# Routing of the first seven tiles in one step, their rows moved from there on, and the weights asked for earlier

## The reference

```python
x = x + _L0_gnn_ref(_layernorm(x), edge_index, edge_type_64, ...)
x = x + _L0_ffn_ref(_layernorm(x)[None], Wr, br, ln_g, ln_b, W1, b1, W2, b2)[0]

def _L0_ffn_ref(x, Wr, br, ln_g, ln_b, W1, b1, W2, b2):
    logits = xt @ Wr + br
    top_p, top_idx = jax.lax.top_k(softmax(logits), 2)
    weights = top_p / top_p.sum(-1)
    xn = (xt - mu) * rsqrt(var + eps)
    h = gelu((xn * ln_g[e] + ln_b[e]) @ W1[e] + b1[e])      # 256 -> 1024, expert e
    y = h @ W2[e] + b2[e]                                   # 1024 -> 256
    out = sum of weights * y over the two chosen experts
```

## Time and profile before

| | |
|---|---|
| median of three runs | 3764.64 us (3761.67 to 3767.57) |
| the profiled execution | 3765.22 us |
| its span, first to last instruction | 3763.4 us |
| PE busy | 2924.2 us (78%) |
| DVE busy | 1675.9 us (45%) |
| ACT busy | 1452.9 us (39%) |
| POOL busy | 1904.0 us (51%) |
| mean granted TensorE clock | 0.872 of full speed |
| step 9 to the first work on block 0 | 2784.67 to 2841.51 us of the trace |

### The profile page before, as it was taken

One profiled execution on the slowest core, in us unless ns is written; L12 is line 12 of the kernel. 1 busy time (PEld: TensorE's weight loads), 2 busy tenths in 40 slices (PEclk: granted clock), 3 DMA queues, 4 the chain that ended last, 5 costly groups with the idle time before them and its releaser, 6 DMA issues. The chain is left out here.

```text
span 3763.4 us, 77621 instructions
## 1 busy us (share of the span) xinstructions
PE 2924.2 (78%) x21213; PEld 2095.5 (56%) x21213; DVE 1675.9 (45%) x6070; ACT 1452.9 (39%) x4666; POOL 1904.0 (51%) x2003
## 2 busy tenths in 40 slices
PE   8687777777777777777777777777757999999998
PEld 7454444444444444444444444444446888889898
DVE  7244444444444444444444444444476554563222
ACT  5343333333333333333333333333335655564332
POOL 6355555555555555555555555555434434432322
PEclk9898888888888888888888888888858999999999
DMA  7566666666666666666666666666476666666665
GB/s 230 165 171 191 184 187 184 190 189 187 184 184 188 189 188 184 187 184 191 188 183 187 184 191 189 185 187 184 138 232 191 200 199 195 197 182 184 188 183 133
DMA packets 295467, 701.49 MB, mean 186 GB/s; under 512 B 47432, under 2 KB 143071, under 8 KB 295188
## 3 DMA queue, kind: packets, MB, share of 16 engines
q0 software_dynamic: 151104, 456.15, 43.5%
q1 hardware_dynamic: 144212, 243.57, 21.2%
HBM read 633.18 MB, written 66.36 MB: 186 GB/s over the span
## 5 line engine op out<-in xcount | busy, mean ns | idle before, releaser
L260 POOL DMA_INDIRECT e_kv<-d_kv,idx x1566 | 1486.4, 949 | 1140.2 <-PE psA L544 690.3
L426 DVE TENSOR_REDUCE e_small<-psD 128x1 f32<-128x384 f32 x261 | 145.5, 557 | 1255.8 <-remote 1250.6
L502 PE MATMUL psK<-consts,e_kv 128*128 128x128 f32 x3132 | 604.3, 316 | 90.8 <-issue 84.2
L353 ACT ACTIVATE e_prob<-psD,e_small 128x384 f32<-128x384 f32 x261 | 151.5, 580 | 1321.4 <-DVE e_small L432 1309.8
L544 PE MATMUL psA<-e_kv,e_probT 128*32 128x128 f32 x6264 | 441.2, 290 | 219.8 <-issue 218.6
L502 PEld LDWEIGHTS psK<-consts,e_kv 128*128 128x128 f32 x3132 | 432.2, 162 | 143.0 <-issue 137.9
L578 PE MATMUL psP<-consts,e_prob 128*128 128x128 f32 x783 | 177.2, 346 | 349.5 <-ACT e_prob L353 349.5
L1600 POOL DMA_INDIRECT out<-f_y,f_whose x105 | 165.8, 1579 | 554.1 <-DVE f_y L1978 387.8
L2146 PE MATMUL f_psY<-f_w,f_hT 128*128 x1680 | 395.1, 389 | 40.0 <-ACT f_hT L1668 34.0
L544 PEld LDWEIGHTS psA<-e_kv,e_probT 128*32 128x32 f32 x6264 | 181.3, 110 | 429.1 <-issue 401.6
L2133 PE MATMUL f_psH<-f_xT,f_w 128*128 128x128 f32 x3360 | 404.3, 280 | 0.9 <-DVE f_xT L1966 0.9
(11 more groups left out here) (309 smaller groups left out, 4108.3 us busy)
## 6 DMA issues: line engine op xcount, KB each, us to landing
f_w<-in_W SPq DMA_DIRECT2D x113, 1024.0 KB
e_rows<-d_feat SPq DMA_DIRECT2D x174, 288.0 KB
e_kv<-d_kv,idx POOLq DMA_INDIRECT x1566
d_accs<-e_accs SPq DMA_DIRECT2D x348, 48.8 KB
f_xs<-d_xs SPq DMA_DIRECT2D x105, 132.5 KB
d_kv<-p_kv SPq DMA_DIRECT2D x48, 256.0 KB, 2.1
p_x<-in_x SPq DMA_DIRECT2D x49, 128.0 KB, 2.8
n_v<-d_kv SPq DMA_DIRECT2D x49, 128.0 KB
```

What stands on the lines that cost most here:

```text
L260: pool.indirect_dma_start(out=kv[g.slot][:, t, :], out_offset=None, in_=kv_dram[:, :], in_offset=bass.IndirectOffsetOnAxis(ap=idx[g.slot][ ...
L502: mm = pe.transpose(psK[:, half, t * P:(t + 1) * P], kv[a.slot][:, third * TS + t, half * P:(half + 1) * P], ident)
```

## The change

Six things move, all in `finish`:

- For the first batch R and S are both laid in step 9 (`FIRST`), in one row of operations, and T in step 10. The later batches stay as they were.
- Its rows are moved in steps 9, 10 and 11 in place of 11, 12 and 13. POOL's gathers of steps 10 and 11 are put behind the moves of step 11.
- ACT's work for the batch (the square root for `r2`, the exponential for `odds`) comes at the end of step 9, and PE's count behind the projection and the turns of step 9.
- W2's eight loads are asked for in steps 2, 3 and 5 to 10 (before: 2, 4, 5, 7, 8, 10, 11, 13).
- W1 of blocks 0, 1 and 2 is asked for in steps 11, 12 and 13, one each (before: all three in step 13), and the rows of block 0 in step 13 (before: 14).
- `PLAIN` goes from 15 to 23, so that in eight more steps PE adds the bias and POOL does not.

```diff
+    placed_at = lambda s: 0 if s == FIRST else batch(s, S_AT) or None
+    listed_at = lambda s: 0 if s == FIRST + 1 else batch(s, T_AT) or None
     R_AT, S_AT, T_AT = 3, 4, 5
-    PLAIN = START
-    W2_AT = {2 + (3 * e + 1) // 2: e for e in range(NX)}
+    FIRST = B - 1 + R_AT
+    LATE = (FIRST + 1, FIRST + 2)
+    PLAIN = START + B + 1
+    W2_AT = {s: e for e, s in enumerate((2, 3, 5, 6, 7, 8, 9, 10))}
...
-            moved.setdefault(k * B + B - 1 + T_AT + j // 3, []).append(k * B + j)
+            moved.setdefault((k * B + B - 1 + T_AT if k else FIRST) + j // 3, []).append(k * B + j)
...
-        weighed.setdefault(START - 2 if b < RW else step_of(b) - 1, []).append(b)
+        weighed.setdefault(LATE[-1] + b if b < RW else step_of(b) - 1, []).append(b)
...
-        fetched.setdefault(step_of(b) - 1, []).append(b)
+        fetched.setdefault(step_of(b) - (1 if b else 2), []).append(b)
...
-                if tile(s + 5) is not None:
+                if tile(s + 5) is not None and s not in LATE:
                     gather(s + 5)
...
+                if s == LATE[-1]:
+                    for g in LATE:
+                        gather(g + 5)
...
+                if k is not None and not here:
+                    second_factor()
+                    gate(k)
                 if not here:
                     sent(s)
...
+                if s == FIRST:
+                    first_rows = itertools.chain(routes, picks, puts)
+                    parts = [sums, itertools.chain(first, then), first_rows, first_rows, first_rows]
...
-                    count(s)
                     project(tile(s))
                     turn(s, 1)
+                    count(s)
```

More of the change, by code:

```diff
@@ L1641, in gate @@
             def gate(k):
+                table(ACT.Exp)
                 act.wait_ge(s_b["R"], (k + 1) * BATCH_OPS["R"])
-                table(ACT.Exp)
                 act.activation(odds[:, 0, :], gap[:, :], ACT.Exp).then_inc(s_gate, 1)
@@ L1696, in _ @@
                 here = BLOCKS_OF.get(s, [])
-                k = batch(s, S_AT)
+                k = placed_at(s)
                 t, b, d, n = tile(s), tile(s - 1), tile(s - 2), tile(s + 1)
@@ L1702, in _, with second_factor @@
                     copied(0, 0)
[L1703 to L1707, removed]
+                def second_factor():
                     now = slice(k * B, k * B + B)
@@ L1710, in _ @@
                     act.activation(r2[:, 2, now], r2[:, 1, now], ACT.Sqrt, bias=cst("eps")).then_inc(s_sd[2], 1)
+                if b is not None or k is not None:
+                    table(ACT.Sqrt)
+                if k is not None and here:
+                    second_factor()
                 if b is not None and here:
@@ L1989, in _ @@
                         pass
[L1990 to L1993, removed]
                 here = BLOCKS_OF.get(s, [])
@@ L2001, in _ @@
                     pass
-                kr, ks, kt = batch(s, R_AT), batch(s, S_AT), batch(s, T_AT)
+                kr, ks, kt = batch(s, R_AT), placed_at(s), listed_at(s)
                 picks = iter(()) if kr is None else chain(s_b["R"], kr * BATCH_OPS["R"], BATCH_OPS["R"], chosen(kr))
```

## The result

| | before | after |
|---|---|---|
| median, 12 runs each on one chip | 3765.39 us (3756.42 to 3770.04) | 3756.11 us (3748.96 to 3761.48) |
| the profiled execution | 3765.22 us | 3752.74 us |
| its span | 3763.4 us | 3750.4 us |
| PE busy | 2924.2 us | 2928.6 us |

The ratio is 0.9976, with a 95% interval from 0.9967 to 0.9985: 9.3 us faster. The forecast was 3758.3 us in a range of 3751 to 3767. It was right in the stage and right in the total, but inside the stage two of its terms were off and cancelled each other, and the term for the bias was wrong.

What follows compares the result with a forecast made beforehand. From step 9 to block 0 no engine is full, so the order of work decides. Terms leave 12.1 us; less 7.0 for late signals, plus 1.2, gives 6.3: median 3764.64 to 3758.3 us, range 3751 to 3767.

Steps and rivals of the forecast that it cites:

- Steps 9 to 11: DVE's steps with R and S together, then T: 12.25, 10.4 and 5.1 us, 27.7 against 26.8, 0.9 lost.
- Rival four: S's wait for PE and ACT in step 9 is 4 us longer: 3762.3 us; chance 0.18 together with rival two.
- The table load: ACT in step 9: 1.28 us with no drain after it; the skill's drain would add some 1.4 us.
- POOL: DVE waits for `alone` of tiles 13 and 14, behind the moves, in steps 12 and 13: 0.8 + 0.4 = 1.2 us.
- The fetch of block 0: Ahead of block 0: asked for in step 13, it no longer waits for the moves, and some 5 us go.
- The late signals: PE's signals to ACT, steps 11 to 14: two of three return beside moves and W1 loads, 2 x 3.5 = 7.0 us.
- Rival three: Signals late in every step with moves beside loads, steps 10 to 14: 14.1 us slower, 3778.7 us; chance 0.09.
- Rival two: All three late signals return, perhaps at a place in ACT's program: 3763.0 us; chance 0.18 together with rival four.
- Rival one: Late signals go altogether, as W1 no longer comes in one 3 MB lump: 12.1 us won, 3752.5 us; chance 0.23.
- The bias: Steps 15 to 22: eight matmuls of 0.20 us on PE in place of POOL's additions, 1.6 us lost.
- W2 in consecutive steps: W2's loads on the DMA queues, 1.71 MB a step: taken as 0; 1.6 us if only 320 GB/s went through.

Runs made afterwards that it cites:

- e1_lump: The changed kernel with W1 of blocks 0 to 2 asked for together in step 13, as before, on the fast chip: 3086.86 us, ratio 0.9975.
- e3_routing_only: The kernel before with only the routing and moves as changed; W1, W2, block 0's fetch and `PLAIN` old; fast chip: 3095.03 us, ratio 1.0006.
- the three kernels of the first group: On the fast chip, the changed kernel with W1 together in step 13, W2's old steps, or W1 together in step 14: 3086.86, 3087.86, 3089.26 us.
- e7_apart: The changed kernel with W1 of blocks 0 to 2 in step 14, behind block 0's fetch, on a slower chip: 3798.48 us, ratio 0.9984.
- e5_plain: The changed kernel with POOL adding the bias from step 15 on, as before (`PLAIN = START`): 3801.59 us, ratio 0.9981.
- after_b: The changed kernel, unchanged, run again for a trace on the chip of the second group of runs: 3799.84 us, ratio 0.9977.

## Why the prediction was right, point by point

**Steps 9 to 11: right in kind, 1.9 us too cheap.** Step 9 was put at 12.25 us and took 13.53 (13.37 to 13.56 in the other traces of the changed order); step 10 at 10.4 and took 10.79; step 11 at 5.1 and took 5.26. Of the 1.28 us in step 9 the rows show 0.66: the wait for the count is 1.19 and not 0.8, and `odds`, costed at nothing, holds DVE for 0.27. The rest lies in no single row. Rival four (4 us more) did not come.

**The table load: the row decided rightly.** The load starts 0.01 us behind the end of ACT's operation before it, and the exponential at 2792.27, 0.02 us behind the load's end at 2792.25. A drain of 1.38 us, which the Trainium skill states in "ScalarE: Activation LUTs", section "What ACT_TABLE_LOAD costs", is not to be seen here; by it the wait of 0.27 would have been some 1.6, an estimate.

**POOL: right, and half as dear.** In the changed kernel's trace the slow stretch covers it: the 0.53 us of idle time ahead of DVE's operation behind `alone` of tile 13 end 0.44 us after `alone` has. `e1_lump`, where nothing is late, shows it: DVE waited 0.32 and 0.30 us for the two, and steps 12 and 13 took 5.32 and 5.47 us, 0.6 us over two plain steps, for 1.2 predicted.

**The fetch of block 0: needed, but on a misread row, and for a reason that I had not priced.** I gave it 5 us, what was left of the 15.9 beside the late signals, and explained it by a wait of 7.8 us for the moves. That wait is the second batch's; the first batch's was 2.75 us, and from its start the rows took 7.9 us to land, 4.27 of them in the transfer. SP came to it only at 2833.50. Ahead of it stood its instructions for the three loads of W1, in pieces of 0.70 us; from the first issue to the last they took 8.59 us, against 2.72 in `e3_routing_only` on the fast chip. How much of the 5 us the earlier fetch won on the first chip no run shows. On the fast chip `e3_routing_only` shows that the other edits hang on it: left in step 14, behind W1, it costs 11.7 us in the stage and 8.2 in the median, where the gain is 7.2. I had named the order on SP but did not price a fetch behind W1.

**The late signals: right in kind, too dear, and with the wrong cause; that the total came out is in part luck.** Without late signals the prediction has 2827.8 - 2783.0 = 44.8 us from step 9 to block 0; the three kernels of the first group with the fetch in step 13 took 46.2 to 46.5 (1.9 us more in steps 9 to 11, 0.6 less for POOL). The changed kernel took 50.75, so its late signals cost 4.4 us (4.9 and 5.4 in the two other traces) where I had 7.0 - 1.2 = 5.8. An error of some +1.5 and one of -1.4 cancel: 50.6 us follow from the prediction, 50.75 were measured, and 7.75 us were won for 7.9 predicted. The 4.4 us do not all stand in "remote": 3.52 do, and the rest in gaps of about 1 us on DVE. As cause I took moves beside megabyte loads, and so that spreading W1 would thin them out; `e7_apart` has a wait of 9.15 us with no such load. I had looked for late signals in `finish` alone: the trace that I read has 254 of them ahead of it, without any move. That the late copies on ACT went from two or three to one, and in `e5_plain` to none, is measured; why is not known. Rival three is out: not five steps of them came. Rival two is out too: not all came back, and they did not stay at a place in ACT's program, for they were the copies of steps 13 and 14 before and of step 12 after. Rival one is what `e5_plain` did in the one execution that was profiled; the changed kernel's own three traces did not.

**The bias: the wrong term.** I counted 1.6 us of loss, one matmul a step on PE, and wrote that nothing urgent waits behind POOL's additions. What counted was what stood beside one of them on DVE: without the additions one step is 0.4 us longer and the next 1.0 shorter, and no cost can be told in the time.

**W2 in consecutive steps: nothing, as predicted.** Steps 3 to 8 took 4.90 to 6.21 us on DVE, each within 0.01 us of what it took before.

In sum 7.9 - 1.6 = 6.3 us were forecast; with the bias at nothing it is 7.8, and the measured 9.3 has an interval of 5.6 to 12.4.

## What to carry to other kernels

When work is pulled forward, follow what takes its result on every queue: on the fast chip, routing two steps earlier won nothing until the first fetch stood ahead of most of the large loads in the queue (14.04 us to land behind 3 MB of W1, and 11.6 us of PE's waiting). An addition on POOL is to be priced by what stands beside it on DVE, and not by POOL's idle time. And cut two spans at the edited stage before believing their difference: 13.0 us here, of which 7.75 lie in the stage, and that stage differed by 4.3 us between two executions on one chip (`after_b` and `e5_plain`) with the same program up to its end.

## What the runs showed of the hardware that was not expected

- The same kernel takes 3094 us on one chip and 3765 to 3811 on others. The DMA queues moved 227 GB/s over the span in `e1_lump`, and 187 in the changed kernel on the first chip. The ratio of the changed kernel is the same on the three chips where it ran, 0.9976, 0.9977 and 0.9977, and `e1_lump` has 0.9975 on the fourth, the fast one.
- In these traces late signals go with the chip first. The fast chip's four have none; on the others DVE waited 1236 to 1295 us for them at one line of the pass over the edges in each trace of the two kernels, more than the 600 us by which that pass is slower. In `finish` those of 1 us and more lie between a batch's first move and 9 us behind POOL's issue of its last. What holds them up stays open.
- A caution on the word "remote": the packed traces of the slower chips hold 31,596 to 32,674 updates of semaphores and those of the fast one 59,015 to 59,133, for nearly the same program, so that the missing names of releasers can come from missing records. The waits themselves are read from starts and ends. Whether taking the profile delays the slower chips was not tested.
- Operations of 0.17 us on DVE with two inputs in SBUF took 0.55 and 0.72 us where POOL had an addition, the second for as long as POOL's lasted.
